# Selection matrices of the first round: one fused operation per chunk, or two broadcast operations per eight chunks

## The chip, the cores and the metric

The kernel runs on one core of a Trainium2 chip. The metric is the device time of one launch in microseconds; lower is better. The engines are named as the profile names them: PE is TensorE (matmul; PEld its weight loads), DVE is VectorE, ACT is ScalarE, POOL is GpSimd, SP is SyncE, which only issues DMAs here.

## The reference

Two graph layers over 12500 nodes of 128 features and 200000 edges, sorted by destination, all in fp32. The first layer has four edge types and two passes over the edges, the second has one pass. That makes three rounds, each of which gathers one row of 128 features for each edge, multiplies it by the edge's weight and adds it to the row of its destination node.

```python
ew = (edge_weight - edge_weight.min()) / (edge_weight.max() - edge_weight.min() + 1e-08)
def _rgcn_conv(x, src, dst, edge_type, edge_weight, W, root, bias):
    xj = x[src]
    m = 0
    for r in range(4):
        mask = (edge_type == r)[:, None]
        m = m + mask * (xj @ W[r])
    m = m * edge_weight[:, None]
    return segment_sum(m, dst, N) + x @ root + bias

h = relu(layernorm(x))
h = relu(_rgcn_conv(h, src, dst, edge_type_4, ew, W1, root1, b1))        # round 1
x = x + _rgcn_conv(h, src, dst, edge_type_4, ew, W2, root2, b2)          # round 2
h = relu(layernorm(x))
x = x + segment_sum(edge_weight[:, None] * h[src], dst, N) @ W.T + b     # round 3
```

## The kernel before

The 200000 edges are cut into chunks of 128 (C = 1563), four chunks make a group (CG), four groups a unit (UG; UC = 16 chunks), so there are 98 units (NU), the last with 11 chunks. A ring of four units (RING) holds the gathered rows in `rows`.

GpSimd gathers. In all three rounds its loop (line 453) issues one indirect DMA for each chunk, which reads 128 row numbers from a column of `idx` and fetches 128 rows of 128 floats. Units 0 to 3 of the first round are fetched from the input x itself while the lists are still being prepared (64 gathers); all others come from a table in HBM. VectorE writes the row numbers into `idx`, for one unit at a time, as soon as TensorE is done with the slots of the ring that they belong to (`take_idx`, lines 1143 to 1150, and `half_idx`, line 1159). From unit 12 on GpSimd's gathers are also paced: the second of each group waits until TensorE has begun the group two before it (`s_begun`).

To sum the rows of a group by destination, TensorE multiplies them by a selection matrix, one for each chunk. In the first round that matrix has RW = 4 x 48 = 192 columns (four edge types, a window of W = 48 destination nodes). Row e of it holds the scaled weight `sw_col` of edge e in the column `key0` = type x 48 + position in the window, and zeros elsewhere. It lies in `wide`, a part of the buffer `win`, that has room for two units. VectorE builds it, one TENSOR_SCALAR for each chunk (line 1200): compare `iota` with the chunk's column of `key0`, then multiply by its column of `sw_col`. TensorE multiplies the 16 chunks of a unit (line 844), ScalarE copies the sums (line 630), TensorE multiplies them by W1 (`mix_unit`, line 762), and VectorE adds the four results to the accumulators (`adds`, line 1081). `add_own0` (line 1088) adds each node's own term.

In rounds two and three the matrix is 48 wide and is built for eight chunks at a time, by `weigh`: an is_equal into PSUM (line 1230), and a mult from there into SBUF (line 1234).

The order of VectorE's work in the first round is written out by hand in `unit` of `first_round`, one step for each group q of unit u. Before the matrices of group 0 it waits until units up to u - 2 are done (`s_half`), for group 2 for `s_own0`, for group 3 for the adds of unit u - 1 (`s_acc`). After group 1 comes the idx copy for unit u + 3, after group 2 the adds of unit u - 1. TensorE waits for the matrices by group: at the last chunk of group g it waits until those of group g + 1 are there (`s_wide`).

Of the kernel before, what the change touches and what calls it, by code (L numbers as in the profile page):

```python
# [4 lines left out]
P = 128  # L5
CG = 4
UG = 4
UC = CG * UG
RING = 4
# [11 lines left out]
def build(nc, x, src, dst, etype, weight, W1, root1, b1, W2, root2, b2, W3, b3, out):  # L21
    fp32, bf16, i32 = mybir.dt.float32, mybir.dt.bfloat16, mybir.dt.int32
    ALU, ACT, AX = mybir.AluOpType, mybir.ActivationFunctionType, mybir.AxisListType.X
# [18 lines left out]
    RW = R * W  # L42
# [18 lines left out]
    with ctx:  # L61
        def sb(name, shape, dt=fp32):
            return ctx.enter_context(nc.sbuf_tensor(name, shape, dt))

        def sem(name):
            return ctx.enter_context(nc.semaphore(name))
# [5 lines left out]
        key_col, rel, key0 = sb("key_col", [P, C]), sb("rel", [P, C]), sb("key0", [P, C])  # L72
        type_col = sb("type_col", [P, C], bf16)
        w_col, sw_col = sb("w_col", [P, C]), sb("sw_col", [P, C])
# [9 lines left out]
        wide = win[:, 0:2 * UC * RW].rearrange("p (a c w) -> p a c w", a=2, w=RW)  # L84
# [20 lines left out]
        iota = sb("iota", [P, RD])  # L105
# [16 lines left out]
        HC = UC // 2  # L122
# [21 lines left out]
        s_tail = [sem(f"s_tail{k}") for k in range(last_chunks)]  # L144
        s_agg, s_acc = sem("s_agg"), sem("s_acc")
        s_begun = sem("s_begun")
        s_idx_part, s_agg_part = sem("s_idx_part"), sem("s_agg_part")

        s_stats, s_mv, s_std, s_rstd, s_shift, s_norm, s_tab = (
            sem(n) for n in ("s_stats", "s_mv", "s_std", "s_rstd", "s_shift", "s_norm", "s_tab"))  # L150
        s_wide, s_half, s_sums, s_mix = (sem(n) for n in ("s_wide", "s_half", "s_sums", "s_mix"))
# [13 lines left out]
        def wait(eng, s, v):  # L165

            if isinstance(v, int) and v <= 0:
                return
            eng.wait_ge(s, v)
# [6 lines left out]
        def first(b, n):  # L176

            return isinstance(b, int) and b < n
# [16 lines left out]
        def groups_of(u):  # L195

            return range(UG) if not isinstance(u, int) else range(min(UG, NG - u * UG))

        def chunks_of(u):

            return UC if not isinstance(u, int) else min(UC, C - u * UC)

        def group_chunks(u, q):

            return CG if not isinstance(u, int) else min(CG, C - (u * UG + q) * CG)
# [9 lines left out]
        def wait_rows(eng, r, u, k):  # L215

            if u == NU - 1:
                eng.wait_ge(s_tail[k], 16 * (r + 1))
            elif k % CG < CG - 1:
                v = u % RING  # L220
                per_round = NI if v < last_units - 1 else NI - 1
                both = 2 if k % CG == CG - 2 else 1
                eng.wait_ge(s_row[v * UG + k // CG][k % CG], 16 * both * (r * per_round + u // RING + 1))
# [715 lines left out]
        def _(eng):  # L939
# [19 lines left out]
            def mean_and_var(e, p, sources):  # L959

                hold(eng, e)
                for k, rows_k in enumerate(sources):
                    ins = eng.bn_stats(stats[0:rows_k.shape[0], p, k, :], rows_k)  # L963
                ins.then_inc(s_stats, 1)
                eng.wait_ge(s_stats, e + 1)
                hold(eng, e)
                for k, rows_k in enumerate(sources):
                    n = rows_k.shape[0]
                    ins = eng.bn_aggr(mv[0:n, p, k, :], stats[0:n, p, k, :])  # L969
                ins.then_inc(s_mv, 1)  # L970

            def scale_and_shift(e, p, n):

                eng.wait_ge(s_std, e + 1)
                eng.reciprocal(rstd[:, p, 0:n], std[:, p, 0:n]).then_inc(s_rstd, 1)
                eng.wait_ge(s_rstd, e + 1)
                eng.scalar_tensor_tensor(out=shift[:, p, 0:n], in0=mv[:, p, 0:n, 0], scalar=-1.0, in1=rstd[:, p, 0:n],
                                         op0=ALU.mult, op1=ALU.mult).then_inc(s_shift, 1)
# [18 lines left out]
            for a, to in ((1, src_col), (2, key_col)):  # L997
                for t in range(MB):
                    n = TURNS.index(a) * MB + t
# [57 lines left out]
            def clear_rest():  # L1057

                eng.wait_ge(s_tabled[1], TABLED[1])
                eng.memset(acc[:, ZB * BT * P:ACC], 0.0).then_inc(s_zero, 1)  # L1060
# [9 lines left out]
            def bases(u, n):  # L1070

                return nc.values_load_multi_w_load_instructions(
                    base_i[0:1, bass.ds(u * UG, n)], engines=(mybir.EngineType.DVE,), min_val=0, max_val=N - 1,
                    skip_runtime_bounds_check_because="the lists name nodes of the graph alone")[1]

            def add(r, g, base, sums_ps):

                a = acc[:, bass.ds(base, W)]
                if r > 0 or g % UG or g < RING * UG:
                    wait(eng, s_acc, g + r * NG)  # L1080
                eng.tensor_tensor(a, a, sums_ps, ALU.add).then_inc(s_acc, 1)  # L1081

            def add_own0(t):

                a = columns(t)
                if not isinstance(t, int) or t == NT - 1:
                    eng.wait_ge(s_own0, t + 1)
                eng.tensor_tensor(a, a, own0_ps[:, 0:P], ALU.add).then_inc(s_own0_add, 1)
# [66 lines left out]
            def half_idx(u, h, signal):  # L1155
# [2 lines left out]
                lo, c = u * UC + h * HC, (u + RING) * UC + h * HC  # L1158
                eng.tensor_copy(idx[:, lo:lo + HC], src_col[:, c:c + HC]).then_inc(signal, 1)

            def first_round():

                def adds(u, v, w):

                    base = bases(u, w)
                    if u == NU - 1:
                        add_own0(u)
                    if first(u, 1):
                        clear_rest()
                        eng.wait_ge(s_zero, 2)  # L1170
                    eng.wait_ge(s_mix, u + 1)
                    if first(u, RING) or u == NU - 1:
                        wait(eng, s_own0_add, u + (u == NU - 1))
                        wait(eng, s_acc, u * UG)
                    for q in range(w):
                        add(0, u * UG + q, base[q], mix_ps[:, q * W:(q + 1) * W])

                def unit(i, v):
                    u = i * RING + v
                    for q in range(UG):  # L1180
                        n = group_chunks(u, q) if q in groups_of(u) else 0
                        g, p = u * UG + q, q % 2
                        raw = n if first(u, RING) else 0
                        if raw:
                            for k in range(n):
                                wait_rows(eng, 0, u, q * CG + k)
                            mean_and_var(NB + g, p, [rows[:, v * UC + q * CG + k, :] for k in range(n)])
                        if n:
                            if q == 0 and not first(u, 2):
                                eng.wait_ge(s_half, u * 2 - 2)  # L1190
                            if q == 1 and not first(u, RING):
                                eng.wait_ge(s_own0_add, u - 1)
                            if q == 2 and not first(u, 1):
                                eng.wait_ge(s_own0, u)
                            if q == 3 and not first(u, 1):
                                eng.wait_ge(s_acc, u * UG)
                                add_own0(u - 1)
                            for k in range(n):
                                c = u * UC + (q * CG + k)
                                ins = eng.tensor_scalar(wide[:, v % 2, q * CG + k, :], iota[:, 0:RW], key0[:, bass.ds(c, 1)],  # L1200
                                                        sw_col[:, bass.ds(c, 1)], ALU.is_equal, ALU.mult)
                            ins.then_inc(s_wide, 1)
                            if raw:
                                scale_and_shift(NB + g, p, n)
                        if q == 0 and 1 <= u <= RING:
                            half_idx(u - 1, 1, s_idx)
                        if q == UG - 1 and u < RING:
                            half_idx(u, 0, s_idx_part)
                        if q == 1 and u > RING and u + RING - 1 < NU:

                            eng.wait_ge(s_half, u * 2)
                            take_idx(u * UC + (RING - 1) * UC, (v - 1) % RING, chunks_of(u + RING - 1))
                        if q == 2 and not first(u, 1):
                            adds(u - 1, v - 1, UG)
                        if q == 3 and not n:
                            eng.wait_ge(s_acc, u * UG)
                            add_own0(u - 1)
                units(unit)
                adds(NU - 1, NU - 1, NG - (NU - 1) * UG)

# [154 lines left out]
```

## Time and profile before

| | us |
|---|---|
| median of 3 runs | 5890.84 |
| lowest and highest | 5890.73, 5891.33 |
| the profiled execution | 5902.65 |
| span in its trace | 5900.5 |

| engine | busy us | share | instructions |
|---|---|---|---|
| PE | 3201.2 | 54% | 11399 |
| PEld | 2549.7 | 43% | 11399 |
| DVE | 1415.0 | 24% | 5035 |
| ACT | 439.7 | 7% | 1183 |
| POOL | 4440.8 | 75% | 4697 |

The span is the time between the first and the last event that the trace holds. The first round lasts until about 1975 us, when the gathers of the second begin; the third begin at about 3938 us. The granted TensorE clock, in tenths of full speed, is mostly 7 or 8 in the first round and 5 from about 2100 us on.

### The profile page before, as it was taken

Reading aid. Unit: us, or ns where it says so; the run is one execution under the profiler, and the core shown is the slowest. Engines: PE = TensorE matmul, PEld = TensorE weight load, DVE = VectorE, ACT = ScalarE, POOL = GpSimd, SP = SyncE. Lnnn points to the kernel's source line nnn. Section 1 sums busy time; section 2 is a strip of 40 time slices with the busy share of each in tenths; the row PEclk is TensorE's granted clock in tenths of the full one; section 3 lists DMA queues with packets and bytes.
Section 4 is the critical chain, followed back from the end, with each engine's and each line's share of the span. In section 5 each row is a group of like instructions: output and inputs, shape, how many; then the busy total and the mean of one; then the engine's idle time right before and its main releaser. Section 6 shows DMA issues by size and latency. Waiting matters only on the chain.

```text
span 5900.5 us, 35868 instructions
## 1 busy us (share of the span) xinstructions
PE 3201.2 (54%) x11399; PEld 2549.7 (43%) x11399; DVE 1415.0 (24%) x5035; ACT 439.7 (7%) x1183; POOL 4440.8 (75%) x4697
## 2 busy tenths in 40 slices
PE   3766666666666544444444444444444444444444
PEld 3645555555555433333333333334444444434343
DVE  7433333333333222112112122121111111111111
ACT  5111111111111000000000000000000000000000
POOL 7777777777777677777777777777777777777777
PEclk7877787778788655555555555555555555555555
DMA  6222222222222222222222222222222222222222
GB/s 171 81 72 72 73 73 72 74 72 71 74 71 73 60 60 58 60 60 58 60 60 58 60 60 58 60 59 58 60 60 58 60 60 60 58 60 60 58 60 58
DMA packets 264681, 390.89 MB, mean 66 GB/s; under 512 B 81547, under 2 KB 176920, under 8 KB 264488
## 3 DMA queue, kind: packets, MB, share of 16 engines
q0 software_dynamic: 150048, 307.60, 20.1%
q1 hardware_dynamic: 114440, 80.97, 4.5%
q8 instruction: 90, 1.47, 0.1%
q14 instruction: 103, 0.84, 0.0%
HBM read 336.91 MB, written 51.34 MB: 66 GB/s over the span
## 4 chain that ended last, share of the span: by engine, by line
POOL 73%; issue 24%; PE 1%; DMA 1%; DVE 1%; ACT 1%; SPq 0%; POOLq 0%; ACTq 0%; DVEq 0%
POOL rows L453 73%; DMA rows<-table,idx 1%; PE bank L844 0%; ACT acc L522 0%; PE bank L784 0%; PE bank L762 0%; SPq L310 0%; DVE stats L963 0%; SPq L299 0%; DVE win L1200 0%; DMA win<-in_edge_type_dram 0%; ACT rows L522 0%; ACT acc L563 0%; PE bank L777 0%; PE bank L792 0%
## 5 line engine op out<-in xcount | busy, mean ns | idle before, releaser
L453 POOL DMA_INDIRECT rows<-table,idx x4625 | 4375.5, 946 | 1430.6 <-issue 1404.6
L885 PE MATMUL bank<-win,rows 128*128 128x48 f32 x6252 | 1859.6, 424 | 2010.9 <-DMA rows<-table,idx 1988.3
L885 PEld LDWEIGHTS bank<-win,rows 128*128 128x128 f32 x6252 | 1508.2, 317 | 2367.3 <-DMA rows<-table,idx 2348.3
L844 PE MATMUL bank<-win,rows 128*128 128x192 f32 x3126 | 864.5, 408 | 647.2 <-DMA rows<-table,idx 503.5
L844 PEld LDWEIGHTS bank<-win,rows 128*128 128x128 f32 x3126 | 607.3, 229 | 857.2 <-DMA rows<-table,idx 680.5
L1200 DVE TENSOR_SCALAR win<-iota,key,sw_col 128x192 f32<-128x192 f32 x1563 | 500.4, 390 | 18.6 <-PE bank L777 16.6
L1081 DVE TENSOR_TENSOR acc<-acc,bank 128x48 f32 x1173 | 237.9, 203 | 1107.5 <-PE bank L762 956.2
L582 ACT ACTIVATE tile_T<-acc 128x128 f32<-128x128 f32 x196 | 60.4, 309 | 2942.7 <-DVE acc L1081 2942.7
L1143 DVE TENSOR_SCALAR idx<-src_col 128x16 int32<-128x16 int32 x98 | 18.2, 189 | 875.7 <-PE bank L885 875.7
L762 PE MATMUL bank<-sums,W1s 128*128 128x192 f32 (+1 forms) x784 | 221.1, 449 | 0.4 <-ACT sums L630 0.4
L1230 DVE TENSOR_TENSOR bank<-bank,rel 128x384 f32<-128x384 f32 x392 | 218.7, 558 | 1.2 <-issue 0.7
L1150 DVE SCALAR_TENSOR_TENSOR idx<-src_col,type_col 128x16 int32<-128x16 int32 x98 | 18.2, 188 | 815.1 <-PE bank L885 815.1
L762 PEld LDWEIGHTS bank<-sums,W1s 128*128 128x128 f32 x784 | 206.0, 281 | 0.9 <-ACT sums L630 0.9
L1131 DVE TENSOR_TENSOR st<-bank,x_rows 128x128 f32<-128x128 f32 x98 | 28.6, 292 | 708.7 <-PE bank L816 708.6
L963 DVE BATCH_NORM_STATS2 stats<-bank 128x6 f32<-128x128 f32 x98 | 29.2, 299 | 681.1 <-PE bank L814 681.1
L784 PE MATMUL bank<-W2s,tile_T 128*128 128x512 f32 x194 | 153.1, 886 | 0.0
L1234 DVE TENSOR_TENSOR win<-bank,sw_col 128x384 f32<-128x384 f32 x196 | 109.0, 556 | 6.8
L1234 DVE TENSOR_TENSOR win<-bank,w_col 128x384 f32<-128x384 f32 x196 | 109.0, 556 | 6.8
L517 ACT ACTIVATE std<-mv,eps 128x1 f32<-128x1 f32 (+3 forms) x127 | 37.2, 293 | 826.4 <-DVE mv L969 826.4
L595 ACT ACTIVATE acc<-bank,b2s 128x128 f32<-128x128 f32 x98 | 36.0, 368 | 781.4 <-PE bank L793 781.4
L792 PEld LDWEIGHTS bank<-tile_T,root2s 128*128 128x128 f32 x194 | 53.0, 274 | 79.2 <-issue 79.2
L630 ACT ACTIVATE sums<-bank 128x384 f32<-128x384 f32 x196 | 85.8, 496 | 5.6 <-PE bank L844 5.6
(110 smaller groups left out, 1117.0 us busy)
## 6 DMA issues: line engine op xcount, KB each, us to landing
rows<-table,idx POOLq DMA_INDIRECT x4625, 2.5
table<-st SPq DMA_DIRECT2D x146, 256.0 KB, 2.3
x_rows<-table SPq DMA_DIRECT2D x49, 128.0 KB, 2.7
x_rows<-in_x_dram SPq DMA_DIRECT2D x48, 128.0 KB, 3.1
h_rows<-table SPq DMA_DIRECT2D x48, 128.0 KB, 2.2
out_dram<-st SPq DMA_DIRECT2D x48, 128.0 KB, 2.1
acc<-in_x_dram SPq DMA_DIRECT2D x13, 448.0 KB, 7.4
table<-acc SPq DMA_DIRECT2D x13, 448.0 KB, 5.8
```

What stands on the lines that cost most here:

```text
L453: eng.indirect_dma_start(out=rows[:, slot, :], out_offset=None, in_=table[:, :], in_offset=bass.IndirectOffsetOnAxis(ap=idx[:, slot:slot + ...
L582: eng.activation(tile_T[:, s, :], columns(t), ACT.Copy).then_inc(s_prep, 1)
L630: eng.activation(sums[:, v % 2, 2 * h:2 * h + w, :].rearrange("p g w -> p (g w)"), half_ps[v % 2 * 2 + h][:, 0:w * RW], ACT.Copy).then_inc ...
L762: ins = eng.matmul(mix_ps[:, 0:w], W1s[:, k, :], rhs(k), start=(k == 0), stop=(k == R - 1))
L784: eng.matmul(wide_of(t)[:, :], inner_of(t, s), W2s[:, :, :].rearrange("p r d -> p (r d)"), start=True, stop=True).then_inc(s_fin, 1)
L792: eng.matmul(own_ps, root2s[:, :], inner_of(t, s), start=True, stop=False)
L844: ins = eng.matmul(half_ps[v % 2 * 2 + h][:, q % 2 * RW:(q % 2 + 1) * RW], chunk_rows(0, u, q * CG + k), wide[:, v % 2, q * CG + k, :], st ...
L885: ins = eng.matmul(agg_of(u, v, q)[:, q * W:(q + 1) * W], chunk_rows(r, u, q * CG + k), window[:, slot, :], start=(k == 0), stop=(k == n - 1))
L1081: eng.tensor_tensor(a, a, sums_ps, ALU.add).then_inc(s_acc, 1)
L1200: ins = eng.tensor_scalar(wide[:, v % 2, q * CG + k, :], iota[:, 0:RW], key0[:, bass.ds(c, 1)], sw_col[:, bass.ds(c, 1)], ALU.is_equal, AL ...
L1230: eng.tensor_tensor(match_ps[:, 0:n, :], iota_ps.unsqueeze(1).to_broadcast([P, n, W]), rel[:, bass.ds(c + lo, n)].unsqueeze(2).to_broadcas ...
L1234: eng.tensor_tensor(slots, match_ps[:, 0:n, :], wt[:, bass.ds(c + lo, n)].unsqueeze(2).to_broadcast([P, n, W]), ALU.mult).then_inc(s_windo ...
```

## The change

In the first round, from unit 4 on, the matrices of eight chunks (half a unit, h = 0 or 1) are built by a new function `weigh_half`. It is called where group 0 and group 2 stood. Its first operation is an is_equal of `iota`, repeated for each chunk, with eight columns of `key0`, each repeated over 192 columns; the result goes to `wide` in SBUF. Its second multiplies that, in place, by eight columns of `sw_col`, each repeated in the same way. A new semaphore, `s_match`, stands between them. `s_wide` then rises by two groups at once. Units 0 to 3 (`raw`) keep the operation for each chunk. Where groups 1 and 3 stood, only their waits, the idx copy and the own term are left.

```diff
+        s_match = sem("s_match")
...
+            def weigh_half(u, v, h):
+
+                lo, n = h * HC, min(HC, chunks_of(u) - h * HC)
+                groups = min(2, groups_of(u)[-1] + 1 - 2 * h)
+                slots = wide[:, v % 2, lo:lo + n, :]
+                c = u * UC + lo
+                eng.tensor_tensor(slots, iota[:, 0:RW].unsqueeze(1).to_broadcast([P, n, RW]),
+                                  key0[:, c:c + n].unsqueeze(2).to_broadcast([P, n, RW]), ALU.is_equal).then_inc(s_match, 1)
+                eng.wait_ge(s_match, (u - RING) * 2 + h + 1)
+                eng.tensor_tensor(slots, slots, sw_col[:, c:c + n].unsqueeze(2).to_broadcast([P, n, RW]),
+                                  ALU.mult).then_inc(s_wide, groups)
...
-                            for k in range(n):
-                                c = u * UC + (q * CG + k)
-                                ins = eng.tensor_scalar(wide[:, v % 2, q * CG + k, :], iota[:, 0:RW], key0[:, bass.ds(c, 1)],
-                                                        sw_col[:, bass.ds(c, 1)], ALU.is_equal, ALU.mult)
-                            ins.then_inc(s_wide, 1)
+                            if raw:
+                                for k in range(n):
+                                    c = u * UC + (q * CG + k)
+                                    ins = eng.tensor_scalar(wide[:, v % 2, q * CG + k, :], iota[:, 0:RW], key0[:, bass.ds(c, 1)],
+                                                            sw_col[:, bass.ds(c, 1)], ALU.is_equal, ALU.mult)
+                                ins.then_inc(s_wide, 1)
+                            elif q % 2 == 0:
+                                weigh_half(u, v, q // 2)
```

VectorE's order in a unit of the first round, in the kernel before; line 1088 is the own term, line 1144 the copy of idx, line 1072 reads the windows' first nodes for the adds of line 1081. The twelve TENSOR_SCALARs are those of group 3 of one unit and groups 0 and 1 of the next.

```order
L1088 TENSOR_TENSOR acc<-acc,bank 128x128
L1200 TENSOR_SCALAR win<-iota,key,sw_col 128x192 x12
L1144 COPY idx<-src_col 128x16
L1200 TENSOR_SCALAR win<-iota,key,sw_col 128x192 x4
L1072 TENSOR_LOAD base_i
```

The same stretch of VectorE in the changed kernel, where the line numbers after the new function are higher:

```order
L1089 TENSOR_TENSOR acc<-acc,bank 128x128
L1168 TENSOR_TENSOR win<-iota,key 128x1536
L1171 TENSOR_TENSOR win<-win,sw_col 128x1536
L1145 COPY idx<-src_col 128x16
L1168 TENSOR_TENSOR win<-iota,key 128x1536
L1171 TENSOR_TENSOR win<-win,sw_col 128x1536
L1073 TENSOR_LOAD base_i
```

The matrices of group 3 have moved from behind the own term to the place ahead of the unit's adds, into the second pair; the first pair is groups 0 and 1 of the next unit. On the other engines nothing moves.

## Rows read from the trace of the kernel before

**Rows 1.** The chain that ended last, by engine (section 4 of the page).
```profile
POOL 73%; issue 24%; PE 1%; DMA 1%; DVE 1%; ACT 1%; SPq 0%; POOLq 0%; ACTq 0%; DVEq 0%
```

**Rows 2.** Page, groups: busy and mean of one, then idle before and its releaser.
```profile
L453 POOL DMA_INDIRECT rows<-table,idx x4625 | 4375.5, 946 | 1430.6 <-issue 1404.6
...
L1200 DVE TENSOR_SCALAR win<-iota,key,sw_col 128x192 f32<-128x192 f32 x1563 | 500.4, 390 | 18.6 <-PE bank L777 16.6
```

**Rows 3.** Busy time by stretch, in round one and in round three.
```profile
core 0: us, PE busy (x) PEld busy (x) DVE busy (x) ACT busy (x) POOL busy (x), PEclk, DMA share, GB/s
500.00:1000.00 500.00, 335.68 (x1225) 258.87 (x1224) 159.15 (x550) 57.41 (x150) 378.32 (x400) 0.80 0.26 72
...
4000.00:5000.00 1000.00, 487.44 (x1700) 403.01 (x1699) 159.97 (x500) 15.45 (x50) 756.07 (x801) 0.50 0.23 59
```

**Rows 4.** Timeline of VectorE in the set-up: start, duration, operation.
```profile
18.93 0.95 DVE L992 CAST win<-win 128x1536 f32<-128x1536 int32 x1
19.80 0.21 DVE L994 CAST win<-win 27x128 f32<-27x128 int32 x1
21.39 0.96 DVE L992 CAST win<-win 128x1536 f32<-128x1536 int32 x1 [1.38 <-DMA win<-in_dst_dram]
...
33.04 1.77 DVE L1013 TENSOR_TENSOR rel<-key_col,base_f 128x1560 f32<-128x1560 f32 x1
...
42.37 1.79 DVE L1026 SCALAR_TENSOR_TENSOR key<-type_col,rel 128x1563 f32<-128x1563 bf16 x1
...
46.48 1.09 DVE L1041 TENSOR_SCALAR sw_col<-w_col,extg,wscale 128x1563 f32<-128x1563 f32 x1
```

**Rows 5.** Timeline of GpSimd in the set-up, the last row unit 4's first gather.
```profile
19.25 1.45 POOL L453 DMA_INDIRECT rows<-in_x_dram,idx  x1 [0.30 <-issue]
21.00 1.47 POOL L453 DMA_INDIRECT rows<-in_x_dram,idx  x1 [0.30 <-issue]
...
32.78 0.95 POOL L453 DMA_INDIRECT rows<-in_x_dram,idx  x1 [0.30 <-issue]
34.04 1.60 POOL L453 DMA_INDIRECT rows<-in_x_dram,idx  x1 [0.30 <-issue]
...
42.20 0.95 POOL L453 DMA_INDIRECT rows<-in_x_dram,idx  x1 [0.30 <-issue]
43.45 1.52 POOL L453 DMA_INDIRECT rows<-in_x_dram,idx  x1 [0.30 <-issue]
...
46.53 1.16 POOL L453 DMA_INDIRECT rows<-in_x_dram,idx  x1 [0.30 <-issue]
...
86.77 0.94 POOL L453 DMA_INDIRECT rows<-table,idx  x1 [0.31 <-issue]
```

**Rows 6.** Timeline of GpSimd, the last gather of round one.
```profile
1962.37 0.95 POOL L453 DMA_INDIRECT rows<-table,idx  x1 [0.31 <-issue]
```

**Rows 7.** Timeline of VectorE in round two, a pair of lines 1230 and 1234.
```profile
2700.05 0.56 DVE L1230 TENSOR_TENSOR bank<-bank,rel 128x384 f32<-128x384 f32 x1
2700.64 0.56 DVE L1234 TENSOR_TENSOR win<-bank,sw_col 128x384 f32<-128x384 f32 x1
```

**Rows 8.** Timeline of one unit of round one, several engines.
```profile
1004.56 1.22 DVE L1081 TENSOR_TENSOR acc<-acc,bank 128x48 f32 x4 [10.76 <-PE bank L762]
...
1006.01 3.68 DVE L1200 TENSOR_SCALAR win<-iota,key,sw_col 128x192 f32<-128x192 f32 x12
...
1006.54 0.96 POOL L453 DMA_INDIRECT rows<-table,idx  x1 [0.31 <-issue]
...
1007.31 1.24 PE L844 MATMUL bank<-win,rows 128*128 128x192 f32 x6 [1.33 <-DVE win L1200]
...
1011.31 0.17 DVE L1144 COPY idx<-src_col 128x16 int32<-128x16 int32 x1 [1.61 <-PE bank L844]
...
1011.53 1.34 DVE L1200 TENSOR_SCALAR win<-iota,key,sw_col 128x192 f32<-128x192 f32 x4
...
1011.56 0.95 POOL L453 DMA_INDIRECT rows<-table,idx  x1 [0.30 <-issue]
```

## The prediction

> **What bounds the kernel now.** I read the chain of waits first. It is GpSimd nearly alone: 73% of the span is the gather of line 453 and 24% is "issue", the time between two gathers in which the queue waits for nothing [rows 1]. The grouped rows give 946 ns for one gather, with 1404.6 of the 1430.6 us before them put down to issue [rows 2]. The stretches of 500 us confirm it: 400 gathers in each, so 1.25 us from start to start, in the first round and, with 801 in 1000 us, in the last one too, where VectorE has quite other work [rows 3]. VectorE is busy for 159 of 500 us in the first round, TensorE for 336. So VectorE's own time is off the path. What counts is whether a VectorE instruction holds up a gather, since each tenth of a microsecond on one of them is added to the end.
>
> **What the set-up shows of this.** Such stops are in the trace, near its start, where large VectorE operations run beside the first 64 gathers. A gather takes 0.94 to 0.96 us when left alone. Reading the two lists side by side [rows 4, 5]:
> - The TENSOR_TENSOR of line 1013 (both inputs in SBUF, 1560 elements) runs from 33.04 to 34.81. The gather that starts at 34.04 takes 1.60 instead of 0.95. If it was stopped at some point and released at 34.81, that point is 35.64 - 34.81 = 0.83 before its end, 0.12 after its start.
> - The SCALAR_TENSOR_TENSOR of line 1026 (two SBUF inputs) runs from 42.37 to 44.16; the gather of 43.45 takes 1.52 and ends 0.81 after that. Again a point about 0.13 after its start.
> - The gather of 32.78 was past its first 0.26 us when line 1013 began, the one of 42.20 past its first 0.17. They take 0.95. So a gather has a short moment, about 0.12 us in, in which a two-input operation stops it, and later it doesn't mind. I take that moment for the reading of its 128 row numbers from idx.
> - The CAST of line 992 at 18.93 (one input, 1536 elements in 0.95 us) stops the gather of 19.25 for 0.50, and the one at 21.39 stops the gather of 21.00 for 0.52, late in it. That is another kind of stop. Line 1041, a TENSOR_SCALAR over 1563 elements, stops the gather of 46.53 for only 0.21.
>
> **The change, part by part.**
> *Removed*: from unit 4 on, 1563 - 64 = 1499 TENSOR_SCALARs of 192 elements, 390 ns each, overlapping to about 0.32 (500.4 us for 1563) [rows 2]. Do they hold up gathers today? Nearly not: 400 gathers in 500 us with twelve and four of them in each unit, as against 801 in 1000 without [rows 3]. From the first gather of unit 4 to the last of the round it is 1962.37 - 86.77 = 1875.6 us for 1498 intervals, 1.2521 each [rows 5, 6]; 1.25 each would be 1872.5. So what can be had back is at most 3 us, and since the clean pace is itself a little over 1.25, I take 2.
> *Added*: in each half unit an is_equal (iota and key0, both in SBUF) and a mult (win and sw_col, both in SBUF), over 8 x 192 = 1536 elements. The nearest row is line 1013, the same instruction with two SBUF inputs: 1.77 us for 1560, so 1.77 x 1536 / 1560 = 1.74 us. 94 units (4 to 97) make 188 pairs. The mult waits for the is_equal through s_match; a pair of this build in round two, lines 1230 and 1234, starts 0.59 apart with 0.56 for one, so the gap is 0.03 to 0.04 [rows 7]. Behind that wait on VectorE stand the copy of idx and the next pair, or the adds, and they lose no more than this gap. VectorE's work in a unit rises from 16 x 0.32 = 5.1 to 4 x 1.74 = 7.0 us, which with its four adds, 1.22, and the index copy, 0.17 [rows 8], makes 8.4 of the 16 x 1.25 = 20 us of a unit. Nothing waits for that.
> *Moved*: the weights of group 3 are made before the adds of the unit before, not after. TensorE waits there today, 1.33 us at 1007.31 for line 1200 [rows 8]; this goes. It gives nothing, because TensorE then waits for the next landing. The next unit's groups 0 and 1 become ready together, at 1006.01 + 3.52 = 1009.5 in the unit shown, and their first matmuls come after the last ones of the unit before, whose end releases the copy of idx at 1011.31 [rows 8]. The copy of idx (line 1144) waits for the end of the unit before, as now, and its numbers are wanted some three units (60 us) later. GpSimd's pacing wait (s_begun) allows TensorE two groups, some 10 us, of lag. No queue but VectorE's is reordered.
>
> **The price of a pair.** A gather reads every 1.25 us. The is_equal lasts 1.74, so it always meets at least one reading. With the reading at x after its start the gather waits 1.74 - x, and x is between 0 and 1.25. It is released at the end of the is_equal. The next reading comes 1.25 later, while the mult runs until 0.04 + 1.74 = 1.78 after that release: 0.53 more. The reading after that is free. In the unit of [rows 8]: first pair, start 1006.01, reading at 1006.54 + 0.12 = 1006.66, waits 1.09 and 0.53. Second pair, start 1011.53, reading at 1011.68, waits 1.59 and 0.53. That would be 3.7 us in this unit.
> Over all units I take x as evenly spread, for the start of a pair hangs on a landing and some matmuls, not on GpSimd: 1.74 - 0.62 = 1.12, with 0.53 it is 1.65 a pair. One row asks for a discount: the gather of 46.53 read at 46.65, 0.17 after line 1041 began, and wasn't stopped then [rows 4, 5]. If an operation takes hold only 0.2 after its recorded start, x lies between 0.2 and 1.45, and the pair costs 0.92 + 0.53 = 1.45. Between 188 x 1.65 = 310 and 188 x 1.45 = 273 I take 291. With 2 us regained it is +289. The profiled execution took 5902.65 us (span 5900.5), 12 more than the median of the runs, 5890.84; in its own terms 6192, as a median 6180.
> Ends: if every pair fell where the wait is shortest (x = 1.45: 0.29 + 0.53 = 0.82), 188 x 0.82 = 154, time 6045. If every pair fell where it is longest (x = 0: 1.74 + 0.53 = 2.27), 427, time 6318.
>
> **Rivals.**
> *VectorE's next instruction goes first.* At the end of the is_equal both the stopped gather and the mult want to go. If the mult won, the gather would wait through it: (1.12 + 1.78) x 188 = 545, time 6435. Against it: after the CAST of 18.93 another follows at 19.80 without any wait, and the gather of 19.25 ends at 20.70, 0.82 after the first CAST's end and 0.69 after the second's; it went on between the two [rows 4, 5]. 8%.
> *No stop at all, and the kernel is not slower.* The stops at 34.04 and 43.45 could belong to something else in the set-up (the index reading of a gather being slow while large transfers run), or a broadcast operand could free the second reader. Then all that is left is what the small operations cost now, 2 us: 5889, no change that can be told. It decides if gathers beside the new lines take 0.95. For it speaks that the gathers of 32.78 and 42.20 ran beside such operations for most of their length at no cost. Against it: two out of two gathers whose 0.12 us point lay inside such an operation were held exactly to its end. 8%, and 2% more for a gain over 0.2%, of which I know no source.
> The Trainium skill, page "SBUF — State Buffer", section "Who interferes with whom", has a sentence for each side. It states that a VectorE instruction with two SBUF inputs contends with a GpSimd instruction that reads SBUF, which agrees with the two stops and gives the forecast; but of DMAs issued by GpSimd it reports that tensor_tensor did not stall them, and infers that making descriptors needs the write side only, which by itself would give this rival's 5889.
> *VectorE or TensorE becomes the bound*, if the four new operations took over (20 - 1.4) / 4 = 4.6 us each instead of 1.74. A pair would then also stop gathers for 4.6 - 0.62 and 4.64 - 1.25 us, 7.4 in all, 188 of them 1390 us: 7280. Line 1013 speaks against it. 2%.
>
> **How the numbers follow.** Forecast case 80%, between 6045 and 6318. VectorE first 8% (6435), no stop 8% (5889), unknown gain 2%, new bound 2%. The range 6045 to 6320 holds 80% and leaves out the others. A measurement of this kernel can tell about 0.2%, 12 us, from no change: faster 0.02, same 0.08, slower 0.90.
>
> **What would show it.** GpSimd's busy time rises by about 290 us, all of it before the second round, with the mean gather there near 1.14 us and rounds two and three as before; the share of issue in us stays. Gathers beside a new pair take 0.95 plus a wait that ends with the is_equal, and the next one about 1.48. Operations of the two new lines take 1.74. TensorE's wait for win goes. Wrong would be: stopped gathers of 2.9 us and more (the mult first), one stop a pair instead of two (then about 170 us), or a pair's start locked to one phase of the gathers, which moves the time within the range.

## The result and the profile after

The changed kernel takes 6241.68 us (median of 4 runs, 6235.35 to 6246.48) against 5891.09 us: a ratio of 1.0593, 95% interval 1.058 to 1.0606. It is slower by 351 us. The forecast was 6180, within 6045 to 6320.

The page of the changed kernel: the span, the engines, the chain that ended last by engine, and the groups of the gather and of the two new lines (busy, mean ns of one | idle before, releaser):

```profile
span 6239.3 us, 35026 instructions
...
PE 3330.6 (53%) x11399; PEld 2662.2 (43%) x11399; DVE 1600.8 (26%) x3912; ACT 439.1 (7%) x1183; POOL 4778.5 (77%) x4697
...
POOL 72%; issue 22%; PE 3%; DMA 1%; DVE 1%; ACT 1%; SPq 0%; POOLq 0%; DVEq 0%; ACTq 0%
...
L454 POOL DMA_INDIRECT rows<-table,idx x4625 | 4712.8, 1019 | 1431.7 <-issue 1400.1
...
L1171 DVE TENSOR_TENSOR win<-win,sw_col 128x1536 f32<-128x1536 f32 x188 | 329.6, 1753 | 20.2 <-DVE win L1168 0.9
L1168 DVE TENSOR_TENSOR win<-iota,key 128x1536 f32<-128x1536 f32 x188 | 329.0, 1750 | 18.7 <-PE bank L778 17.3
```

Read it against [rows 1, 2]. The bound is the same, gathers one after the other. There are still 4625 of them, and the time between them is the same (1431.7 against 1430.6 us). But they are busy for 4712.8 instead of 4375.5 us, 337 more, which is nearly all of the 339 by which the span grew. Both figures are a little too small for the change: the profiled execution of the kernel before ran 12 us over its median, with gathers of 0.9458 us in rounds two and three as well, against 0.9435 in the changed kernel. The new operations take 1.75 us each, as worked out from line 1013.

The busy time by stretch, round one and round three, shows where:

```profile
core 0: us, PE busy (x) PEld busy (x) DVE busy (x) ACT busy (x) POOL busy (x), PEclk, DMA share, GB/s
500.00:1000.00 500.00, 307.82 (x1038) 239.07 (x1036) 177.11 (x212) 48.66 (x128) 397.29 (x338) 0.75 0.22 61
...
4500.00:5500.00 1000.00, 487.58 (x1700) 403.49 (x1700) 160.02 (x500) 15.45 (x50) 755.78 (x802) 0.50 0.23 59
```

In 500 us of round one 338 gathers are made where [rows 3] had 400; in round three 802 in 1000, against 801. All of the loss is in the first round.

One unit of it, on the timelines of VectorE and of GpSimd (start, duration, operation):

```profile
1012.66 1.75 DVE L1168 TENSOR_TENSOR win<-iota,key 128x1536 f32<-128x1536 f32 x1
1014.52 1.76 DVE L1171 TENSOR_TENSOR win<-win,sw_col 128x1536 f32<-128x1536 f32 x1
...
1020.89 1.76 DVE L1168 TENSOR_TENSOR win<-iota,key 128x1536 f32<-128x1536 f32 x1
1022.75 1.76 DVE L1171 TENSOR_TENSOR win<-win,sw_col 128x1536 f32<-128x1536 f32 x1
```
```profile
1011.76 0.94 POOL L454 DMA_INDIRECT rows<-table,idx  x1 [0.30 <-issue]
1013.01 2.22 POOL L454 DMA_INDIRECT rows<-table,idx  x1 [0.30 <-issue]
1015.53 1.56 POOL L454 DMA_INDIRECT rows<-table,idx  x1 [0.30 <-issue]
1017.40 0.94 POOL L454 DMA_INDIRECT rows<-table,idx  x1 [0.31 <-issue]
...
1021.15 2.31 POOL L454 DMA_INDIRECT rows<-table,idx  x1 [0.30 <-issue]
1023.76 1.56 POOL L454 DMA_INDIRECT rows<-table,idx  x1 [0.30 <-issue]
```

The gather of 1013.01 takes 2.22 and ends at 15.23, which is 0.82 after the end of the is_equal (1012.66 + 1.75 = 1014.41). The next one ends at 1017.09, 0.81 after the end of the mult (1016.28). The third takes 0.94. The second pair does the same, with 2.31 and 1.56. That is the pattern of the forecast: two stops in a pair, each until the operation ends, and the third gather free.

### The profile page after: what moved, and what is told of

It reads as the page before. It is cut to its first block, busy times and chain, and to the rows that moved or that the text cites. A ratio compares the mean times of both kernels' runs of the same rounds, so it can differ in the third digit from the quotient of the medians.

```text
span 6239.3 us, 35026 instructions
## 1 busy us (share of the span) xinstructions
PE 3330.6 (53%) x11399; PEld 2662.2 (43%) x11399; DVE 1600.8 (26%) x3912; ACT 439.1 (7%) x1183; POOL 4778.5 (77%) x4697
## 4 chain that ended last, share of the span: by engine, by line
POOL 72%; issue 22%; PE 3%; DMA 1%; DVE 1%; ACT 1%; SPq 0%; POOLq 0%; DVEq 0%; ACTq 0%
POOL rows L454 72%; PE bank L845 1%; DMA rows<-table,idx 1%; PE bank L763 1%; ACT acc L523 0%; ACT rows L523 0%; DVE stats L964 0%; DVE win L1214 0%; SPq L311 0%; PE bank L785 0%; SPq L300 0%; DMA win<-in_edge_type_dram 0%; PE bank L771 0%; ACT acc L564 0%; DVE mv L970 0%
## 5 line engine op out<-in xcount | busy, mean ns | idle before, releaser
L454 POOL DMA_INDIRECT rows<-table,idx x4625 | 4712.8, 1019 | 1431.7 <-issue 1400.1
L886 PEld LDWEIGHTS bank<-win,rows 128*128 128x128 f32 x6252 | 1510.3, 318 | 2358.5 <-DMA rows<-table,idx 2339.4
L845 PE MATMUL bank<-win,rows 128*128 128x192 f32 x3126 | 927.6, 430 | 863.1 <-DMA rows<-table,idx 791.0
L845 PEld LDWEIGHTS bank<-win,rows 128*128 128x128 f32 x3126 | 657.7, 247 | 1077.4 <-DMA rows<-table,idx 991.6
L1171 DVE TENSOR_TENSOR win<-win,sw_col 128x1536 f32<-128x1536 f32 x188 | 329.6, 1753 | 20.2 <-DVE win L1168 0.9
L1168 DVE TENSOR_TENSOR win<-iota,key 128x1536 f32<-128x1536 f32 x188 | 329.0, 1750 | 18.7 <-PE bank L778 17.3
L763 PE MATMUL bank<-sums,W1s 128*128 128x192 f32 (+1 forms) x784 | 254.6, 501 | 0.4 <-ACT sums L631 0.4
L763 PEld LDWEIGHTS bank<-sums,W1s 128*128 128x128 f32 x784 | 239.9, 322 | 0.9 <-ACT sums L631 0.9
L785 PE MATMUL bank<-W2s,tile_T 128*128 128x512 f32 x194 | 174.6, 1003 | 0.0
L1145 DVE COPY idx<-src_col 128x16 int32<-128x16 int32 x90 | 28.6, 318 | 353.4 <-PE bank L845 353.4
```

The costliest lines, as they stand in the source:

```text
L454: eng.indirect_dma_start(out=rows[:, slot, :], out_offset=None, in_=table[:, :], in_offset=bass.IndirectOffsetOnAxis(ap=idx[:, slot:slot + ...
L763: ins = eng.matmul(mix_ps[:, 0:w], W1s[:, k, :], rhs(k), start=(k == 0), stop=(k == R - 1))
L785: eng.matmul(wide_of(t)[:, :], inner_of(t, s), W2s[:, :, :].rearrange("p r d -> p (r d)"), start=True, stop=True).then_inc(s_fin, 1)
L845: ins = eng.matmul(half_ps[v % 2 * 2 + h][:, q % 2 * RW:(q % 2 + 1) * RW], chunk_rows(0, u, q * CG + k), wide[:, v % 2, q * CG + k, :], st ...
L886: ins = eng.matmul(agg_of(u, v, q)[:, q * W:(q + 1) * W], chunk_rows(r, u, q * CG + k), window[:, slot, :], start=(k == 0), stop=(k == n - 1))
L1168: eng.tensor_tensor(slots, iota[:, 0:RW].unsqueeze(1).to_broadcast([P, n, RW]), key0[:, c:c + n].unsqueeze(2).to_broadcast([P, n, RW]), AL ...
```

## The experiments

The question after the result was not whether gathers are stopped, but what stops them, and why a pair costs 351 / 188 = 1.87 us and not 1.55.

**What stops them.** First the mult and then both operations were replaced by TENSOR_REDUCEs of the same length. They have one SBUF input.

```diff
-                eng.tensor_tensor(slots, slots, sw_col[:, c:c + n].unsqueeze(2).to_broadcast([P, n, RW]),
-                                  ALU.mult).then_inc(s_wide, groups)
+                eng.tensor_reduce(gtmp[:, 0:1], slots, axis=mybir.AxisListType.XY, op=ALU.max).then_inc(s_wide, groups)
```

> The mult of each pair is replaced by a TENSOR_REDUCE over the same 1536 elements, which has one SBUF input; the is_equal stays. So the weights are left out of the first round's matrices. Theory (an operation with two SBUF inputs holds a gather at the point where it reads idx, until the operation ends): the first stopped gather of each pair waits 1.24 us as in the changed kernel, the second is free: 188 x 1.24 = 233, about 6125 us. Rival (any long VectorE operation, or one that reads win, stops gathers): as the changed kernel, about 6240. Second rival (the stop comes from the in-place mult): near 5895.

Measured: 6095.13 us, ratio 1.0345 (1.0324 to 1.0365), 202 us over the kernel before. The timelines of one pair:

```profile
1010.09 1.75 DVE L1168 TENSOR_TENSOR win<-iota,key 128x1536 f32<-128x1536 f32 x1
1010.53 2.13 POOL L454 DMA_INDIRECT rows<-table,idx  x1 [0.30 <-issue]
1011.94 1.75 DVE L1171 TENSOR_REDUCE gtmp<-win 128x1 f32<-128x1536 f32 x1
1012.96 0.94 POOL L454 DMA_INDIRECT rows<-table,idx  x1 [0.30 <-issue]
```

The gather beside the is_equal is held to 0.82 past its end; the one beside the reduce takes 0.94. Over the 188 pairs the stopped gathers lose 1.07 us each (worked out from the intervals between gathers), not the 1.24 assumed, which is why the time is 30 us under the expectation. With other work behind it the is_equal meets the gathers at other places: in 21 pairs the first gather goes free and the next is held for less, in the changed kernel in 2.

> Both operations of each pair are replaced by TENSOR_REDUCEs over the same 1536 elements with one SBUF input each. The first round's matrices are then not built from unit 4 on. VectorE's busy time stays as in the changed kernel. Theory: no gather is stopped, 5889 to 5892 us, and no gather in the first round after unit 4 takes over 1.1 us. Rival (VectorE's time or the later order of its work sets the end): near 6240, or at least well above 5891.

Measured: 5893.02 us, ratio 1.0 (0.9989 to 1.001). The groups of the gather and of the two reduces:

```profile
L454 POOL DMA_INDIRECT rows<-table,idx x4625 | 4365.5, 944 | 1431.1 <-issue 1406.4
L1170 DVE TENSOR_REDUCE gtmp<-win 128x1 f32<-128x1536 f32 x188 | 328.5, 1747 | 20.0 <-DVE gtmp L1168 0.9
L1168 DVE TENSOR_REDUCE gtmp<-win 128x1 f32<-128x1536 f32 x188 | 327.8, 1744 | 20.0 <-PE bank L778 18.9
```

VectorE is as busy as in the changed kernel, in the same places and for the same stretches, and nothing is lost. So neither its time nor long operations as such are the cause, but the kind of operation. The two kernels differ in the number of SBUF inputs, in the name of the operation, in the operand that is repeated (broadcast) over 192 columns, and in what it writes (one column instead of 1536). That it is the inputs rests on rows of the kernel before: the SCALAR_TENSOR_TENSOR of line 1026 has two in SBUF, neither repeated, and held a gather [rows 4, 5]; lines 1230 and 1234 are TENSOR_TENSORs with one input in PSUM and one, repeated, in SBUF, line 1234 writes 384 columns to SBUF, and of the 208 gathers in rounds two and three that are at their point of 0.12 us in the middle of such an operation (0.17 us or more after its start) none takes over 0.96 us.

This does not make every operation with one tensor from SBUF harmless. The gather of 19.25 ends 0.82 us after the end of the CAST of line 992 (18.93 + 0.95 = 19.88) [rows 4, 5], so it was held at the same point as the others; only the gather of 21.00, which ends 0.12 after the end of its CAST, and the one of 46.53, 0.12 after the end of line 1041, were stopped late in their course. The prediction called all of this another kind of stop.

**The new order of work alone.** Eight TENSOR_SCALARs at the places of groups 0 and 2.

```diff
...
+                for k in range(n):
+                    ins = eng.tensor_scalar(slots[:, k, :], iota[:, 0:RW], key0[:, c + k:c + k + 1],
+                                            sw_col[:, c + k:c + k + 1], ALU.is_equal, ALU.mult)
+                ins.then_inc(s_wide, groups)
```

> The new order of work alone: eight chunks' matrices at a time at the places of groups 0 and 2, but each with its TENSOR_SCALAR as before. Theory (the stops of the new operations are all of the loss, and TensorE's wait for the matrices was off the path): TensorE's 1.3 us waits for win go, and the time is that of the kernel before within 0.1%, 5888 to 5895 us. Rival (the later or larger portions cost time themselves): clearly above 5895.

Measured: 5891.75 us, ratio 1.0 (0.9991 to 1.0009). Its list of waits in the first round (us in total, times, longest):

```profile
PE bank L845 <- DMA rows<-table,idx: 568.7, 587, 3.1
...
PE bank L845 <- DVE win L1169: 8.7, 5, 1.9
```

In the kernel before the same list has these rows:

```profile
PE bank L844 <- DMA rows<-table,idx: 503.5, 490, 3.0
PE bank L844 <- DVE win L1200: 84.8, 72, 2.0
```

76 us of TensorE's waits for the matrices are gone, its waits for landings have grown by 65, and the time is the same. The wait was off the path.

The TENSOR_SCALARs do hold gathers, but seldom and briefly. In this kernel and in the kernel before, 16 of the 1499 gathers from unit 4 on take 0.97 to 1.06 us, 1.4 and 1.2 us more in all than 0.945 each. Every one of them ends 0.81 to 0.83 us after the end of a TENSOR_SCALAR that had begun 0.24 to 0.34 us before the gather's point. The operation lasts about 0.38 us, so little is left of it by then.

**Length of the operations.** The same pairs, on two chunks and then on one at a time.

```diff
+                step = 2
+                done = ((u - RING) * 2 + h) * (HC // step)
+                for k in range(0, n, step):
+                    m, part = min(step, n - k), slots[:, k:k + min(step, n - k), :]
+                    eng.tensor_tensor(part, iota[:, 0:RW].unsqueeze(1).to_broadcast([P, m, RW]),
+                                      key0[:, c + k:c + k + m].unsqueeze(2).to_broadcast([P, m, RW]), ALU.is_equal).then_inc(s_match, 1)
+                    eng.wait_ge(s_match, done + k // step + 1)
+                    ins = eng.tensor_tensor(part, part, sw_col[:, c + k:c + k + m].unsqueeze(2).to_broadcast([P, m, RW]), ALU.mult)
+                ins.then_inc(s_wide, groups)
```

> The same broadcast pairs, but for two chunks at a time (384 elements), four pairs to each half unit, all with two SBUF inputs. Theory (a gather waits only for the rest of the operation that it meets, so the cost of a meeting grows with the operation's length): an operation is about 0.56 us, a half unit takes about 4.2 us and meets 3.4 readings of 0.18 to 0.28 us wait each: 0.6 to 0.95 us, times 188 = 113 to 179, so 6004 to 6070 us. Rival (the cost goes with the time in which such operations run, 1.86 us for 3.5 us as in the changed kernel): 4.2 us cost 2.2, 188 x 2.2 = 414, about 6305 us.

Measured: 5977.09 us, ratio 1.0141 (1.0122 to 1.0161).

> The broadcast pairs for one chunk at a time (192 elements, eight pairs to a half unit), two SBUF inputs each. An operation is about 0.36 us and can stop a gather in its last 0.2, one starts every 0.33, a half unit takes 5.3 us and meets 4.2 readings: 4.2 x 0.6 x 0.1 = 0.26 us, times 188 = 50: about 5945 us, less than the 5977 of the pairs of two chunks although VectorE is busy for longer. Rival (cost goes with the busy time of two-input operations): more than the 85 us of two chunks, 5.3 / 4.2 x 85 = 107, about 6000 us.

Measured: 5957.73 us, ratio 1.0111 (1.0095 to 1.0126). The groups of the first operation of a pair, and VectorE's whole busy time, for two chunks and then for one:

```profile
L1172 DVE TENSOR_TENSOR win<-iota,key 128x384 f32<-128x384 f32 x750 | 413.2, 551 | 13.9 <-PE bank L778 13.3
...
PE 3243.5 (54%) x11399; PEld 2590.1 (43%) x11399; DVE 1727.6 (29%) x5036; ACT 438.9 (7%) x1183; POOL 4511.4 (76%) x4697
```
```profile
L1172 DVE TENSOR_TENSOR win<-iota,key 128x192 f32<-128x192 f32 x1499 | 528.7, 353 | 16.0 <-PE bank L778 16.0
...
PE 3221.9 (54%) x11399; PEld 2541.5 (43%) x11399; DVE 1894.7 (32%) x6534; ACT 439.6 (7%) x1183; POOL 4474.3 (75%) x4697
```

With eight, two and one chunk to an operation the loss is 351, 84 and 66 us, while VectorE's busy time rises from 1600.8 to 1727.6 and 1894.7. In the last of these, 20 us have nothing to do with held gathers (timelines of GpSimd and, below the dots, of TensorE):

```profile
250.42 1.02 POOL L454 DMA_INDIRECT rows<-table,idx  x1 [0.30 <-issue]
270.38 0.94 POOL L454 DMA_INDIRECT rows<-table,idx  x1 [18.94 <-PE bank L845]
...
260.80 1.01 PE L845 MATMUL bank<-win,rows 128*128 128x192 f32 x2 [4.71 <-DVE win L1175]
```

The gather of 270.38 is the second of unit 12, the first that is paced by TensorE. TensorE is still behind there and waits itself for the matrices. Of the chain of waits between 225 and 275 us, 57% are VectorE's two new lines: here VectorE's time is on the path, once. What the gathers themselves take over 0.945 us adds up to 349, 81 and 44 us in the three kernels. So what a hold costs is not the time in which such operations run but the time that is left of one when a gather comes to read. Two chunks cost less than the lowest value expected (6004); the holds of one chunk, 44 us, are close to the 50 expected, and the wait of 18.94 us was in no expectation.

**Where in the is_equal the reading falls.** A TENSOR_REDUCE of one input ahead of each is_equal, first over 600 elements.

```diff
+                eng.tensor_reduce(gtmp[:, h:h + 1], rel[:, 0:600], axis=AX, op=ALU.max)
                 eng.tensor_tensor(slots, iota[:, 0:RW].unsqueeze(1).to_broadcast([P, n, RW]),
```

> The changed kernel with a TENSOR_REDUCE over 600 elements (one SBUF input, about 0.78 us, some 0.7 of it as a shift) ahead of each is_equal. More work, later matrices. Theory (the wait is the end of the is_equal less the time of the reading, and the pairs start at a nearly fixed 0.86 to 0.92 us after a gather's start): the start moves to about 0.35 us after the next gather's start, just past its reading at 0.12, the next reading is 1.05 us into the is_equal and waits 0.7 instead of 1.25. The pair costs 1.3 instead of 1.86: 188 x 0.55 = 103 less, about 6140 us. Rival (starts are spread evenly, or the wait doesn't depend on them): 6240 or a little more.

Measured: 6180.9 us, ratio 1.0489 (1.0468 to 1.051). More work and 61 us less, where 100 were expected. In the trace the first stop of a pair costs 0.93 us on average instead of 1.24, 59 us less in 188 pairs, and the second costs 0.62 in both kernels. So the gain is the place of the reading in the is_equal. Then the same over 200 elements.

> As the delay before, but with a TENSOR_REDUCE over only 200 elements ahead of each is_equal, which shifts it by some 0.28 us instead of 0.7. Theory (the wait is the is_equal's end less the reading's time): readings come 0.28 us earlier in the is_equal, 0.23 instead of 0.51 after its start, and wait 0.28 longer, up to 53 us more, less what falls under the 0.15 us in which an operation doesn't hold yet: 6260 to 6295 us, so a shorter delay costs and the longer one gained 60. Rival (the delay of 0.7 gained for another reason, as less crowding of VectorE's work): between 6181 and 6242 us.

Measured: 6215.58 us, ratio 1.0553 (1.0537 to 1.0569). This expectation failed: the time fell by 26 us instead of rising by 20 to 50. Two pairs of this kernel show why (timelines of VectorE and GpSimd):

```profile
1000.55 0.94 POOL L454 DMA_INDIRECT rows<-table,idx  x1 [0.30 <-issue]
1000.66 1.75 DVE L1169 TENSOR_TENSOR win<-iota,key 128x1536 f32<-128x1536 f32 x1
1001.80 1.42 POOL L454 DMA_INDIRECT rows<-table,idx  x1 [0.30 <-issue]
...
1014.91 1.75 DVE L1169 TENSOR_TENSOR win<-iota,key 128x1536 f32<-128x1536 f32 x1
1015.37 2.10 POOL L454 DMA_INDIRECT rows<-table,idx  x1 [0.30 <-issue]
```

The gather of 1000.55 comes to its reading 0.01 us after the is_equal's recorded start and isn't held; the next one loses 0.48. The one of 1015.37 reads 0.58 in and loses 1.16. I took the place of the reading (gather's start + 0.12) in all 188 pairs of three kernels. In the changed kernel its median is 0.47 us after the start of the is_equal, in this one 0.20, as meant. But a gather whose reading falls less than 0.148 us after the start slips through in every pair of the six kernels that have an is_equal over 1536 elements, and one from 0.17 us on is held in every pair, but for the short last operation of the round; in between both happen. Of the 188 pairs, 2 slip through in the changed kernel and 46 here. These lose 0.42 us at their first stop, the 142 others 1.33. Had the 46 lost that too, the time would be 46 x 0.91 = 42 us more, about 6258; the expectation had allowed for this only in words, not in its number. The time of a single held gather follows the rule: its end lies 0.80 to 0.83 us after the is_equal's in 997 of 998 cases in six kernels. The spread of the pairs' starts was what wasn't known well enough.

A gather that just slips through does the same to VectorE, on a small scale: beside readings 0.12 to 0.15 us after its start the is_equal takes 1.79 to 1.82 us instead of 1.75.

**What moves the pairs' starts.** In the changed kernel 162 of 188 readings fall between 0.30 and 0.60 us, near the dear end; spread evenly over 1.25 us it would be 45. VectorE's adds, which come ahead of the first pair, wait for the eight matmuls of mix. In the kernel before these take 1.46 us in 21 of 81 units and over 2.6 in 37, and the adds begin 4.9 and 6.8 us (medians) after the start of the unit's eighth gather. In the changed kernel they take over 2.6 us in 65 of 79 units, and the adds begin at 6.90 with 6.82 and 7.04 as the ends of that group. So the fast units are gone, and with them most of the spread. The granted clock of the first round went down too, 0.74 against 0.80. As a trial TensorE was given more to do, matmuls against zeros, which add nothing to the sums:

```diff
+                                for _ in range(0 if raw or k == 0 else 1):
+                                    eng.matmul(half_ps[v % 2 * 2 + h][:, q % 2 * RW:q % 2 * RW + P], chunk_rows(0, u, q * CG + k),
+                                               zeros[:, :], start=False, stop=False)
```

> The changed kernel with extra work on TensorE alone: from unit 4 on, each of the chunks 1 to 3 of a group adds one matmul against the zeros tile (128 columns) to its open group, 12 more in a unit. Question: is the place at which the pairs start among the gathers set by TensorE's granted clock? In the changed kernel the eight matmuls of mix take 2.77 us in 65 of 79 units and the adds start 6.9 us after the unit's eighth gather; in the kernel before, units whose mix takes 1.46 us have the adds at 4.9. Theory: where the clock stays high the adds come at 4.9, which puts the is_equal's start 0.02 ahead of a reading, too late to hold that one (it holds from 0.15 on), so the next one waits 0.5 instead of 1.25 us. If half of the first pairs get there, 49 x 0.7 = 35 us less; if all, 70 less: 6170 to 6210 us. Rival (the phase has another origin, or TensorE's time counts): 6240 or more.

> The same with two such matmuls for each of these chunks, 24 more in a unit, some 5 us at the high clock. Theory: more units keep the high clock and the time falls further or as far as with one, 6165 to 6205 us, as long as TensorE doesn't become the bound (14.8 us busy of 23.5 in a unit, with this about 20). Rival (TensorE's time counts, or the phase has another origin): 6240 or more, rising with the number of matmuls.

Measured: 6203.65 us (ratio 1.0529, 1.0508 to 1.055) with one, 6193.73 us (1.0508, 1.0487 to 1.0528) with two. The first round by stretch in the changed kernel, with one and with two:

```profile
110.00:2320.00 2210.00, 1389.92 (x4720) 1084.07 (x4720) 809.38 (x1074) 237.79 (x624) 1747.74 (x1483) 0.74 0.22 61
```
```profile
110.00:2280.00 2170.00, 1500.68 (x6962) 1262.04 (x6961) 794.91 (x1065) 236.15 (x618) 1709.57 (x1482) 0.81 0.23 62
```
```profile
110.00:2280.00 2170.00, 1617.69 (x9220) 1422.82 (x9220) 800.36 (x1080) 238.66 (x627) 1707.15 (x1485) 0.89 0.24 63
```

TensorE has 111 and 228 us more to do, its granted clock rises to 0.81 and 0.89, and the kernel gets 38 and 48 us faster, because the gathers are held for less: over 0.945 us each they take 349, 310 and 307 us in the three kernels. The direction and the size came out as expected, the working did not. The mix now takes 1.46 us in 21 and 62 units, but starts later behind the added matmuls, and the adds come at 5.4 and 5.8 us, not 4.9. The first pairs lose as much as before (1.13 and 1.16 us at the first stop, against 1.19); the second pairs lose 0.93 and 0.86 against 1.29. It is their readings that have moved, from 0.45 us after the start of the is_equal (median) to 0.80 and 0.85. Shown is that TensorE's timing changes how dear a pair is. That the adds and the first pairs' starts follow from the clock is not shown: it was the reason for the trial, and the first pairs did not get cheaper. How much of it is the clock and how much the added matmuls' own time was not separated.

## Why the prediction was right, and where it was off

- *The bound, and that VectorE's and TensorE's times don't count*: right. The run with both operations of one input has VectorE's 1592.8 us and the time of before; the new order alone gives it too. The run of one chunk shows the limit: there 18.94 us of one wait go back to VectorE.
- *A gather has a moment, 0.12 us in, at which a two-input operation holds it*: right to the hundredth. The held gathers of the timelines end 0.81 to 0.82 after the operation. That this moment is the reading of the row numbers is the prediction's interpretation, and this text uses the word; no run has a GpSimd DMA that reads none, so it is not shown.
- *Two stops in a pair, the gather goes ahead of the mult*: right, and with it the rival of 6435 us falls: in six kernels 997 of 998 gathers held by an is_equal are free at its end, before the operation behind it. *No stop at all* (5889 us) falls too, as does the sentence of the Trainium skill, page "SBUF — State Buffer", section "Who interferes with whom", that would have given it: the statement that a tensor_tensor did not stall GpSimd's DMAs does not hold for these gathers, which read their row numbers from SBUF. Its other rule, of two SBUF inputs against a GpSimd instruction that reads SBUF, agrees with every trace here.
- *The second stop*: 0.53 expected, 0.62 measured. The mult begins 0.105 us after the is_equal's end in these pairs and not 0.035; in the unit shown, 1014.52 - 1014.41 = 0.11. 0.07 to 0.08 us in 188 pairs are 14 us, and the operation itself is 0.01 longer. The released gather is not the cause of the wider gap. With TENSOR_REDUCEs in both places, where no gather is held, the median gap is 0.103 us too, and with pairs of two chunks or of one it is 0.035 whether a gather is held or not. The gap goes with operations of 1536 elements, and the prediction had taken it from a pair of 384.
- *The first stop* is the term that was mis-sized. The discount was right in size: a two-input operation holds from about 0.15 us after its recorded start (0.2 was one end, 0 the other). The row that it came from was partly luck, for line 1041 is a TENSOR_SCALAR, and the small ones of the first round hold only from 0.24 us on. What failed is the step "over all units I take x as evenly spread". With x between 0.15 and 1.40 it gives 0.97 us a pair; measured are 1.24. The starts recorded before the change, taken as they were, would have given 288 us in all with the measured 0.15 and 0.105, so they are no better: the change moved the starts themselves.
- *289 forecast, 351 measured*: the 291 us of the forecast are 188 x (1.02 + 0.53). The first stop measured 1.24, which is 42 us more, the second 0.62, 16 us more. With the 2 us that did not come back that makes 60 of the 62.
- *Removed operations*: 2 us were taken as regained. The trace before has 1.2 us of holds by them, too little to be told from the measurement.
- *The sum of two stops in a pair* closes in the other kernels too. 188 times the measured stops are 202 us for a loss of 202 without the mult, 291 and 324 for 288 and 324 with the two delays, 311 and 307 for 312 and 302 with the added matmuls.

## What to carry to other kernels

If GpSimd issues indirect DMAs back to back and is the bound, look in VectorE's rows for operations with two inputs in SBUF: each can hold a gather to its end. Fewer and longer ones are then dearer than many short ones. TENSOR_TENSORs with one input in PSUM and TENSOR_REDUCEs cost nothing here. A long CAST or TENSOR_SCALAR from SBUF is not free (0.50 and 0.21 us of one gather in the set-up), a TENSOR_SCALAR of 192 elements nearly so. Before costing such a stop by an even spread, see whether the two engines are tied to each other through landings, as here, where 162 of 188 readings fell into a quarter of the gathers' period. Small additions of work on VectorE or TensorE, neither of which is the bound, can then move the total by tens of microseconds: here they made the changed kernel faster by 26 to 61 us.

## What the runs showed of the hardware beyond expectation

- The hold is sharp. A gather that comes to its reading less than 0.148 us after the recorded start of a two-input operation goes free (0.94 us); from 0.17 us on it waits for the end (2.5 us in all). In 1128 pairs of six kernels (the changed one, the one without the mult, the two delays, the two with added matmuls) nothing but the short last operation of the round departs from this; between the two figures 3 gathers go free and 28 are held. A gather that has just got in lengthens VectorE's operation by up to 0.08 us.
- A TENSOR_SCALAR with scalars from SBUF and 192 elements (391 ns) holds a gather only from 0.24 us after its start, for 0.12 us at most: 16 of 1499 gathers, 1.4 us in the run of the new order. Beside 188 pairs of TENSOR_REDUCEs of 1536 elements no gather is held.
- A CAST of 1536 elements held one gather at its point of 0.12 us, and another late in its course, which ended 0.12 us after the CAST. Two-input operations do the first alone: 346 gathers of the six kernels were 0.83 us in while an is_equal had been running for 0.17 us or more, and none of them took over 0.96 us.
- Twelve and 24 added matmuls in a unit made the kernel faster, by 38 and 48 us, through the places at which two other engines meet.
